# A 512-column clear on GpSimd behind each of the 3616 indirect transfers of a graph network kernel

## The chip, the cores and the metric

One Trainium2 chip, one core of it. The metric is the device time of one execution in microseconds. The engines are TensorE (PE; its weight loads are PEld in the profile), VectorE (DVE), ScalarE (ACT), GpSimd (POOL) and SyncE (SP). Two kernels are compared, before and after one change.

## The reference

A graph of 12500 nodes with 32 features and 200000 edges, sorted by destination. Layer 0 is an equivariant message layer: for each edge a small network of its weight gives 384 numbers R, which are multiplied with the features of the edge's source node and with directions, and summed at the edge's destination. Three graph convolutions follow. Cut to the core:

```python
h = jnp.maximum(_layernorm(x, axis=-1), 0.0)
# layer 0
R = jax.nn.relu(abs_distances[:, None] @ w1 + b1) @ w2 + b2
Fj = features[src]
acc = acc + _NORM[i] * jnp.einsum('euv,ef,evi,ofi->euo', Rb[..., k], Yf, Fb, C)
out = out.at[dst].add(msg)
x = x + out
# layers 1 to 3, on maximum(layernorm(x), 0)
h = x @ W
msg = h[src] * norm[:, None]
out = jax.ops.segment_sum(msg, dst, num_segments=n_nodes)
x = x + relu(conv3(relu(conv2(relu(conv1(h))))))
```

## The kernel before, in words

Each layer n keeps the node rows that its edges read in a table in DRAM, `tables[n]`, of 32, 96, 128 and 96 columns (float32 in layers 0 and 2, bfloat16 in 1 and 3). The edges are cut into groups of 1024. GpSimd fetches the source rows of a group with eight indirect transfers of 128 rows each (L768), one for each column of the index tile `idx`, into one of four slots of the buffer `rows`. These eight are called a block here. Layer 0 fetches all 196 groups so (`GATHERED[0]`); layers 1, 2 and 3 fetch 92, 100 and 64 groups, 452 in all, 3616 transfers. The other edges of layers 1 to 3 are taken as "buckets" by matmuls with one-hot matrices out of tables in SBUF (PE L2051, L2066, L2069; DVE L1597, L1626; ACT L987, L991), which run between the groups.

What a group is used for: in layer 0, ACT copies the fetched rows out of the slot (L864 to L871, the last one counts the semaphore `rows_copied`), PE makes R (L1908, L1911), DVE multiplies (L1336, L1344, L1354) and PE sums the messages with a one-hot matrix of destinations (L1926). DVE then adds the result into `accT` (L1382). In layers 1 to 3 PE sums the rows of a group directly (L2137, semaphore `group_summed`) and DVE adds them into `accT` (L1750).

The order of the work is written out by hand for each engine. `sweep` makes a first pass, a `Fori` loop over the passes between, and a last pass, peeled off on both sides; a pass holds 4 groups in layer 0, and 12, 12 and 8 in layers 1 to 3. GpSimd runs `gathers(n)`: for each group u it waits for the indices of its slot (`idx_in`, loaded by SP), then for the group four before, which used the same slot, to be read (`rows_copied` in layer 0, `group_summed` in the others), and issues the eight transfers, each counting `gathered`. So it may be up to four groups ahead. Each layer's transfers start when its table is written. SP reloads a slot's indices when `gathered` says that the transfers of that slot have landed. In the first pass of layer 0, GpSimd also clears `accT` behind its 32 transfers (L775, 12672 columns), and DVE's first addition into `accT` needs that.

The semaphore `made` counts GpSimd's constants; all who wait for it wait for at most 9.

```python
pool.wait_ge(rows_copied[r], pool.snap(turn[r]) + 1)
pool.reg_add(turn[r], turn[r], 1)
for j in range(TPG):
    col = j % 2 * KS + j // 2
    (pool.indirect_dma_start(..., tables[n], bass.IndirectOffsetOnAxis(ap=idx[:, r, col:col + 1], axis=0))
         .then_inc(gathered[r], 16))
```

Of the kernel before, what the change touches and what calls it, by code (L numbers as in the profile page):

```python
# [27 lines left out]
P = 128  # L28
# [8 lines left out]
TPG = 8  # L37
# [21 lines left out]
MSGW = TAIL0 + OUTS  # L59
SUMW = 8 * OUTS  # L60
PAD_REL = -1000.0
assert NG % UNROLL == 0 and PTAIL * KS == ETAIL and PTAIL <= P and NG == 2 * NB


# [2 lines left out]
GATHERED = [NG, 92, 100, 64]  # L67
LOOP = [(UNROLL, 0), (12, 10), (12, 8), (8, 12)]
# [64 lines left out]
def gnn_kernel(nc, x, src, dst, edge_attr, edge_weight, w1, b1, w2, b2,  # L133
               W1, B1, W2, B2, W3, B3, out):
    ctx = ExitStack()
    with ctx:
        def sb(name, shape, dt=fp32):
            return ctx.enter_context(nc.sbuf_tensor(name, shape, dt))
# [4 lines left out]
        def sem(name):  # L143
            return ctx.enter_context(nc.semaphore(name))
# [147 lines left out]
        far_shift = sb("far_shift", [P, NB + 1])  # L292
        ident = sb("ident", [P, P])
        one = sb("one", [P, 1])
        flag = sb("flag", [P, 1])
        w1c = sb("w1c", [P, 1])
        b1c = sb("b1c", [P, 1])
# [34 lines left out]
        made = sem("made")  # L332
# [118 lines left out]
        def rounds_before(n):  # L451

            return sum(GATHERED[:n]) // UNROLL
# [87 lines left out]
        def sweep(eng, body, n=0):  # L541

            body(Step(eng, 0, n), True, False)
            with eng.Fori(1, ITS[n] - 1) as it:
                body(Step(eng, it, n), False, False)
            body(Step(eng, ITS[n] - 1, n), False, True)
# [181 lines left out]
        @block.gpsimd  # L728
        def _(pool):
            nc.gpsimd.memset(xn[:, NB - 1, :], 0.0).then_inc(pads, 1)  # L730
            pool.wait_ge(pads, 1)
            nc.gpsimd.memset(attr_rows[96:NB, 1, :], 1.0).then_inc(pads, 1)
            pool.wait_ge(pads, 2)
            nc.gpsimd.iota(iota_i[:, :], pattern=[[1, WIN]], base=0, channel_multiplier=0).then_inc(made, 1)
            nc.gpsimd.iota(line_i[:, :], pattern=[[0, 1]], base=0, channel_multiplier=1).then_inc(made, 1)
            nc.gpsimd.iota(far_shift_i[:, :], pattern=[[WIN, NB + 1]], base=0, channel_multiplier=0).then_inc(made, 1)
            nc.gpsimd.memset(ident[:, :], 0.0).then_inc(made, 1)
            nc.gpsimd.memset(one[:, :], 1.0).then_inc(made, 1)
            nc.gpsimd.memset(ew_row[:, :, :], 0.0).then_inc(made, 1)
            nc.gpsimd.memset(idx[:, :, :], 0).then_inc(made, 1)  # L740
            nc.gpsimd.memset(ones_h[:, :], 1.0).then_inc(made, 1)
            pool.wait_ge(made, 8)
            nc.gpsimd.affine_select(out=ident[:, :], in_=ident[:, :], compare_op=ALU.not_equal, fill=1.0,
                                    base=0, pattern=[[-1, P]], channel_multiplier=1).then_inc(made, 1)

            turn = [pool.alloc_register(f"turn_pool{u}") for u in range(UNROLL)]

            def gathers(n):  # L750
                def body(step, first, last):
                    for u in range(shape(n, last)[0]):
                        r, use = u % UNROLL, u // UNROLL
                        pool.wait_ge(idx_in[r], step.times(step.groups // UNROLL * 16, 16 * (rounds_before(n) + use + 1)))
                        if n > 0:
                            if step.peeled and (not first or use):
                                pool.wait_ge(*when(group_summed, step, u - UNROLL, before=convs_before(n)))
                            elif not step.peeled:
                                pool.wait_ge(group_summed[r % 2], pool.snap(turn[r]) + (2 * convs_before(n) + r // 2 + 1))
                                pool.reg_add(turn[r], turn[r], 2)  # L760
                        elif last:
                            pool.wait_ge(rows_copied[r], step.it * (step.groups // UNROLL) + use)
                        elif not first:
# [4 lines that stand above are left out]
                            (pool.indirect_dma_start(rows_3[:, r, j, :] if n in (1, 3) else rows[:, r, j, 0:WIDTH[n]], None, tables[n],  # L768
                                                     bass.IndirectOffsetOnAxis(ap=idx[:, r, col:col + 1], axis=0))
                                 .then_inc(gathered[r], 16))  # L770
                    if n == 0 and first:
                        pool.wait_ge(centred, 2)
                        nc.gpsimd.memset(xn[:, NB - 1, :], 0.0).then_inc(pads, 1)
                        pool.wait_ge(prepared, 1)
                        nc.gpsimd.memset(accT[:, :], 0.0).then_inc(acc_cleared, 1)  # L775
                        pool.wait_ge(directed, 1)
                        nc.gpsimd.memset(src_b[:, (NBG - 1) * BJ:NBG * BJ], NO_SOURCE).then_inc(pads, 1)
                        nc.gpsimd.memset(dst_b[:, (NBG - 1) * BJ:NBG * BJ], -1).then_inc(pads, 1)
                if n < 2:
                    pool.wait_ge(table_out[n], 48 if n == 0 else 32)  # L780
                else:
                    if n == 3:
                        for c in range(NCH):
                            bs = blocks_of(c)
                            pool.wait_ge(middle_made, thirds_before(3) + c + 1)
                            nc.gpsimd.tensor_tensor(thirds3[:, bs, 2 * F:F3], lnA[:, bs, :], thirds3[:, bs, F:2 * F],
                                                    ALU.subtract).then_inc(thirds_made, 1)
                    for c in range(NCH - 4, NCH):
                        pool.wait_ge(chunk_out[c % 4], chunks_stored(n, c))
                for u in range(UNROLL):  # L790
                    pool.reg_mov(turn[u], 2 * (LOOP[n][0] // UNROLL - 1) if n else 0)
                sweep(pool, body, n)

            for n in range(NLAYER):
                gathers(n)
# [304 lines left out]
        def _(dve):  # L1100
# [104 lines left out]
            for n in range(4):  # L1205
# [4 lines left out]
                                     mins_by[:, h, w, :].unsqueeze(1).to_broadcast([P, KS, NB]), ALU.subtract))  # L1210
            link(v.tensor_scalar(pad_line, line[:, :], float(PTAIL), PAD_REL, ALU.is_ge, ALU.mult))
            link(v.tensor_scalar(rel_of[:, 1, 0, :, NB - 1], rel_of[:, 1, 0, :, NB - 1], pad_line, None, ALU.add))
            link(v.memset(rel_of[:, 1, 1, :, NB - 1], PAD_REL))

# [1052 lines left out]
```

## Time and profile before

| | us |
|---|---|
| median of 3 runs | 8061.44 |
| lowest and highest run | 8028.29, 8071.3 |
| the profiled execution, first to last instruction (span) | 8083.0 |
| TensorE busy | 5256.2 (65%) |
| VectorE busy | 3618.0 (45%) |
| ScalarE busy | 2730.5 (34%) |
| GpSimd busy | 3513.2 (43%) |
| mean granted TensorE clock | 0.721 |

The profiled execution's own time is known as its span alone, 8083.0 us; it lies 0.3% above the median of the three runs. "Busy" is the time in which an engine executes; in "idle before" stands what released it. "issue" means that the engine waited for nothing that the profile shows; "remote" and "another core or an unknown queue", that the releaser's record is missing. The granted clock is the share of full speed that TensorE was given. A row for GpSimd's transfer covers the making of its descriptors, not the moving of the data.

### The profile page before, as it was taken

To read this page: it belongs to the slowest core of one execution; us is meant where nothing else is said; L and a number is where in the kernel's file an instruction comes from. 1 tells how busy PE (TensorE), PEld (TensorE's weight loads), DVE (VectorE), ACT (ScalarE), POOL (GpSimd) and SP (SyncE) were. 2 spreads that over 40 slices of the span, in tenths; PEclk is the share of its full clock that TensorE was granted. 3 is DMA by queue.
4 is the path that set the end of the run, shared out by engine and by line. 5 is a ranking of instruction groups with operands and counts; after the bars stand their busy time and mean duration, and the time that the engine had idled before them with its cause. 6 is when DMAs were issued, how large, how long until landed. Compare 5 with 4: busy or idle time off the path is not lost.

```text
span 8083.0 us, 169450 instructions
## 1 busy us (share of the span) xinstructions
PE 5256.2 (65%) x62463; PEld 3511.6 (43%) x62464; DVE 3618.0 (45%) x8469; ACT 2730.5 (34%) x6550; POOL 3513.2 (43%) x3660
## 2 busy tenths in 40 slices
PE   4777677776767775554544557777777778455555
PEld 2444344443434443333333345555555556333333
DVE  6666566665656656444444442222222223333334
ACT  3333333333333333444444432222222223222222
POOL 5545445444444542444444434333333332444442
PEclk8877788787877776555555567887777788565566
DMA  2111111111111113222222221111111112222223
GB/s 66 26 26 27 24 26 27 26 26 24 27 24 26 26 25 37 59 55 55 55 55 55 55 80 55 57 56 53 56 55 53 55 55 83 68 79 81 78 82 87
DMA packets 494908, 400.37 MB, mean 50 GB/s; under 512 B 269575, under 2 KB 454828, under 8 KB 493537
## 3 DMA queue, kind: packets, MB, share of 16 engines
q10 hardware_dynamic: 146996, 207.67, 7.6%
q0 software_dynamic: 115712, 109.02, 7.1%
q1 hardware_dynamic: 231536, 74.48, 4.2%
q8 instruction: 459, 7.52, 0.4%
q14 instruction: 205, 1.68, 0.1%
HBM read 375.52 MB, written 15.29 MB: 48 GB/s over the span
## 4 chain that ended last, share of the span: by engine, by line
PE 38%; another core or an unknown queue 22%; DVE 18%; issue 17%; ACT 2%; DVEq 1%; DMA 1%; ACTq 0%; SPq 0%
PE radial L2051 14%; PE sums L1926 5%; DVE scratch L1344 4%; DVE scratch L1336 4%; PE sums L2137 4%; PE psX L2066 3%; PE psT L2066 3%; PE radial L1911 2%; PE psX L2069 2%; DVE scratch L1354 2%; PE psT L2069 1%; DVE shared L1310 1%; PE radial L2033 1%; PE radial L1908 1%
## 5 line engine op out<-in xcount | busy, mean ns | idle before, releaser
L768 POOL DMA_INDIRECT rows<-table,idx x3616 | 3486.8, 964 | 4415.6 <-PE sums L2137 2099.7
L2051 PE MATMUL radial<-arena,shared 128*32 128x96 bf16 (+1 forms) x31200 | 1469.7, 283 | 1072.6 <-issue 907.8
L2051 PEld LDWEIGHTS radial<-arena,shared 128*32 128x32 bf16 (+1 forms) x31200 | 848.1, 120 | 1551.6 <-issue 1311.4
L1926 PE MATMUL sums<-scratch,onehot 128*64 128x264 f32 (+1 forms) x9408 | 1134.5, 393 | 378.2 <-DVE scratch L1361 207.2
L1926 PEld LDWEIGHTS sums<-scratch,onehot 128*64 128x64 f32 x9408 | 818.2, 161 | 924.6 <-issue 480.7
L834 ACT ACTIVATE dist<-iota,rel 128x64 f32<-128x64 f32 (+1 forms) x2368 | 619.5, 342 | 1190.4 <-PE sums L1926 790.0
L1597 DVE TENSOR_SCALAR shared<-scratch,line 128x640 bf16<-128x640 bf16 (+1 forms) x906 | 408.3, 451 | 1367.9 <-remote 1102.7
L991 ACT CAST scratch<-radial 128x480 bf16<-128x480 f32 x860 | 470.8, 556 | 1593.4 <-remote 985.1
L1911 PE MATMUL radial<-shared 64*128 64x384 f32 x3136 | 880.9, 583 | 81.4 <-issue 77.8
L1336 DVE TENSOR_TENSOR scratch<-radial,shared 128x512 f32<-128x512 f32 x784 | 536.4, 684 | 740.4 <-remote 704.1
L1344 DVE TENSOR_TENSOR scratch<-radial,shared 128x768 f32<-128x768 f32 x784 | 741.6, 946 | 0.0
L987 ACT COPY scratch<-radial 128x384 f32<-128x384 f32 x350 | 167.3, 478 | 1275.4 <-remote 824.9
L1908 PE MATMUL radial<-shared 64*128 64x384 bf16 x1568 | 304.2, 370 | 403.2 <-DVE scratch L1344 239.6
L1626 DVE TENSOR_TENSOR shared<-radial,shared 128x480 bf16<-128x480 bf16 x860 | 345.0, 402 | 354.3 <-remote 231.3
L857 ACT ACTIVATE shared<-shared,b1c,w1c 128x512 f32<-128x512 f32 x196 | 256.9, 1311 | 657.1 <-remote 642.3
L1911 PEld LDWEIGHTS radial<-shared 64*128 64x128 f32 x3136 | 371.7, 222 | 206.1 <-issue 203.5
L1623 DVE TENSOR_TENSOR shared<-iota,shared 128x480 f32<-128x480 f32 x350 | 230.1, 657 | 394.9 <-remote 182.3
L2069 PE MATMUL psT<-shared,scratch 128*96 128x96 bf16 x2150 | 252.7, 271 | 203.0 <-issue 107.9
L2069 PE MATMUL psX<-shared,scratch 128*96 128x96 bf16 x2150 | 242.8, 264 | 187.3 <-issue 107.7
L1908 PEld LDWEIGHTS radial<-shared 64*128 64x128 bf16 x1568 | 81.9, 96 | 648.3 <-issue 321.1
L2137 PE MATMUL sums<-onehot,rows 128*128 128x80 f32 (+1 forms) x2844 | 346.5, 286 | 25.9 <-issue 24.9
L2137 PEld LDWEIGHTS sums<-onehot,rows 128*128 128x128 f32 (+1 forms) x2844 | 310.3, 196 | 77.3 <-issue 65.6
(236 smaller groups left out, 5445.4 us busy)
## 6 DMA issues: line engine op xcount, KB each, us to landing
scratch<-places_d ACTq DMA_DIRECT2D x242, 800.0 KB
rows<-table,idx POOLq DMA_INDIRECT x3616
shared<-in_edge_weight SPq DMA_DIRECT2D x390, 128.0 KB
idx<-in_src SPq DMA_DIRECT2D x451, 4.0 KB
table<-arena SPq DMA_DIRECT2D x24, 256.0 KB, 2.7
table<-arena SPq DMA_DIRECT2D x2, 1176.0 KB, 10.6
accT<-in_edge_attr SPq DMA_DIRECT2D x2, 1152.0 KB
table<-arena SPq DMA_DIRECT2D x24, 96.0 KB, 2.0
```

What stands on the lines that cost most here:

```text
L768: (pool.indirect_dma_start(rows_3[:, r, j, :] if n in (1, 3) else rows[:, r, j, 0:WIDTH[n]], None, tables[n], bass.IndirectOffsetOnAxis(ap ...
L834: ins = nc.scalar.activation(dist[:, j, 0:span], iota[:, 0:span], ACT.Abs, scale=-1.0, bias=rel[:, bass.ds(step.tile(u) + j, 1)])
L991: nc.scalar.copy(taken[n][:, h, :, :], radial[0][:, h, 0:KC * F3].rearrange("p (t f) -> p t f", f=F3)).then_inc(bucket_copied, 1)
L1336: prod = v.tensor_tensor(msg[:, h, t:t + 2, 0:2 * SEG0].rearrange("p t (m s) -> p t m s", s=16), R[:, :, 0:256].rearrange("p t (m s) -> p ...
L1344: last = v.tensor_tensor(msg[:, h, t:t + 2, SEG0 + 16 * (MUL + 1):TAIL0].rearrange("p t (n s) -> p t n s", s=16), R[:, :, 256:384].unsquee ...
L1908: nc.tensor.matmul(radial[q % 2][:, k, 0:RDIM], ones_h[half, :], bias_rows[half, :], start=True, stop=False, tile_position=(k * HID0, 0))
L1911: last = nc.tensor.matmul(radial[q % 2][:, k, 0:RDIM], hid[half, u % 2, q, :], w2n[half, 0, :], start=False, stop=True, tile_position=(k * ...
L1926: last = nc.tensor.matmul(there, onehot[:, u % 2, 4 * h + t, 0:SW], taken_from, start=(h + q + part == 0), stop=(h == 1 and q == 1 and par ...
L2051: last = nc.tensor.matmul(d, from_src[n][:, h, i, t, :], table_of(n, s), start=True, stop=True, tile_position=(0, 32 * i))
L2066: last = nc.tensor.matmul((psX if v % 2 else psT)[0:BWIN, 0:HID], to_dst[n][:, h, t, :], taken[n][:, h, t, :], start=(c + t == 0), stop=(c ...
L2069: last = nc.tensor.matmul((psX if v % 2 else psT)[0:w, 0:BWIN], taken[n][:, h, t, :], to_dst[n][:, h, t, :], start=(c + t == 0), stop=(c * ...
L2137: mm = nc.tensor.matmul(sums[0:w, u % 2, 0:CWIN], far_rows[j], (onehot if n == 2 else onehot_3)[0:counts[j], u % 2, j, 0:CWIN], start=(j = ...
```

## The change

Behind each indirect transfer GpSimd now clears a buffer of its own, `pause`, of 512 float32 columns. Every clear counts `made`, and waits for the clear before it: in the peeled passes for a constant, in the loops for a register that is counted up. Nobody reads `pause`.

```diff
+PAUSE = 512
...
+        pause = sb("pause", [P, PAUSE])
...
+            pauses = pool.alloc_register("pauses")
+
+            def pause_between(step, n, u, j):
+
+                if step.peeled:
+                    before = TPG * (sum(GATHERED[:n]) + step.it * step.groups + u) + j
+                    if before:
+                        pool.wait_ge(made, 9 + before)
+                else:
+                    pool.wait_ge(made, pool.snap(pauses))
+                    pool.reg_add(pauses, pauses, 1)
+                nc.gpsimd.memset(pause[:, :], 0.0).then_inc(made, 1)
...
                                  .then_inc(gathered[r], 16))
+                            pause_between(step, n, u, j)
...
+                pool.reg_mov(pauses, 9 + TPG * (sum(GATHERED[:n]) + LOOP[n][0]))
                 sweep(pool, body, n)
```

The instructions of PE, DVE, ACT and SP stand in the same order as before. Those of GpSimd change in all passes alike: a clear follows each transfer. In GpSimd's loop of layer 0 they stood so before, a row for each kind of instruction, with the semaphores waited for in brackets:

```order
L764 ISA [waits idx_in0]
L765 REGISTER_ALU [waits rows_copied0]
L768 DMA rows<-table,idx 128x32 x8
L764 ISA [waits idx_in1]
L765 REGISTER_ALU [waits rows_copied1]
L768 DMA rows<-table,idx 128x32 x8
```

and now, for the first half of one block (L764 to L768 of before are L778 to L782 here):

```order
L778 ISA [waits idx_in0]
L779 REGISTER_ALU [waits rows_copied0]
L782 DMA rows<-table,idx 128x32
L761 REGISTER_ALU [waits made]
L762 MEMSET pause 128x512
L782 DMA rows<-table,idx 128x32
L761 REGISTER_ALU [waits made]
L762 MEMSET pause 128x512
L782 DMA rows<-table,idx 128x32
L761 REGISTER_ALU [waits made]
L762 MEMSET pause 128x512
```

Between two transfers of a block stand now one register addition, one wait and one clear. At the end of the first pass of layer 0, ahead of the long clear of `accT`, it is:

```order
L782 DMA rows<-table,idx 128x32
L762 MEMSET pause 128x512 [waits made]
L782 DMA rows<-table,idx 128x32
L762 MEMSET pause 128x512 [waits made]
L788 MEMSET xn 128x32 [waits centred]
L790 MEMSET accT 128x12672 [waits prepared]
```

All 32 clears of the first four blocks stand ahead of the clear of `accT`.

## Rows read from the trace of the kernel before

**Rows 1.** The page: busy time by engine, and the chain's shares by engine
```profile
PE 5256.2 (65%) x62463; PEld 3511.6 (43%) x62464; DVE 3618.0 (45%) x8469; ACT 2730.5 (34%) x6550; POOL 3513.2 (43%) x3660
...
PE 38%; another core or an unknown queue 22%; DVE 18%; issue 17%; ACT 2%; DVEq 1%; DMA 1%; ACTq 0%; SPq 0%
```

**Rows 2.** GpSimd's transfers at 130:3050, 3168:4690, 4778:6770, 6888:8015; busy us, mean ns | idle
```profile
L768 POOL DMA_INDIRECT rows<-table,idx x1498 | 1439.3, 961 | 1482.0 <-ACT shared L871 1040.6 <-issue 441.4
...
L768 POOL DMA_INDIRECT rows<-table,idx x732 | 710.9, 971 | 920.4 <-PE sums L2137 604.2 <-issue 206.9 <-DMA table<-arena 109.4
...
L768 POOL DMA_INDIRECT rows<-table,idx x793 | 771.1, 972 | 1303.3 <-PE sums L2137 995.9 <-issue 307.4
...
L768 POOL DMA_INDIRECT rows<-table,idx x505 | 476.9, 944 | 654.7 <-PE sums L2137 499.6 <-issue 148.7 <-remote 6.4
```

**Rows 3.** Stretches: PE, PEld, DVE, ACT, POOL busy us (instructions), clock, DMA share, GB/s
```profile
79.70:90.30 10.60, 8.52 (x74) 5.55 (x76) 10.36 (x19) 8.91 (x24) 10.60 (x2) 1.00 0.21 54
90.60:96.60 6.00, 5.78 (x49) 3.26 (x45) 5.82 (x10) 4.43 (x13) 4.72 (x5) 1.00 0.16 35
96.60:130.50 33.90, 7.40 (x31) 3.74 (x30) 2.62 (x7) 0.95 (x4) 25.64 (x27) 0.60 0.11 18
130.50:160.00 29.50, 21.52 (x153) 12.51 (x152) 20.81 (x39) 10.99 (x33) 7.07 (x8) 0.82 0.34 78
```

**Rows 4.** The same view inside one block each of layers 0, 1, 2 and 3
```profile
1044.00:1049.00 5.00, 4.82 (x44) 3.29 (x42) 5.00 (x9) 2.74 (x9) 3.77 (x4) 1.00 0.12 18
1049.00:1055.20 6.20, 3.13 (x18) 1.55 (x14) 2.42 (x4) 2.93 (x7) 3.77 (x4) 1.00 0.19 48
...
3914.80:3922.40 7.60, 1.72 (x14) 0.91 (x14) 0.86 (x3) 0.56 (x1) 4.79 (x5) 0.59 0.16 28
...
5568.20:5571.90 3.70, 3.23 (x61) 2.58 (x60) 0.82 (x2) 0.00 (x0) 2.86 (x3) 1.00 0.47 152
5571.90:5579.50 7.60, 3.57 (x22) 0.90 (x21) 0.55 (x1) 0.75 (x2) 4.85 (x5) 0.71 0.19 52
5579.50:5588.20 8.70, 8.47 (x87) 7.38 (x88) 2.11 (x4) 4.51 (x14) 0.00 (x0) 0.67 0.02 1
...
7317.00:7325.70 8.70, 2.45 (x21) 1.23 (x21) 1.05 (x3) 0.56 (x1) 5.66 (x6) 0.63 0.28 78
```

**Rows 5.** Two blocks of layer 2 in order of time: start, us, what [idle before]
```profile
5510.19 0.97 POOL L768 DMA_INDIRECT rows<-table,idx  x1 [11.73 <-PE sums L2137]
5512.98 0.94 POOL L768 DMA_INDIRECT rows<-table,idx  x1 [1.82 <-issue]
...
5568.20 0.97 POOL L768 DMA_INDIRECT rows<-table,idx  x1 [11.78 <-PE sums L2137]
5569.48 0.94 POOL L768 DMA_INDIRECT rows<-table,idx  x1 [0.31 <-issue]
...
5516.55 0.27 PE L2051 MATMUL radial<-arena,shared 128*32 128x128 f32 x1 [0.33 <-issue]
...
5572.46 0.45 PE L2051 MATMUL radial<-arena,shared 128*32 128x128 f32 x5 [1.02 <-issue]
```

**Rows 6.** ACT in order of time, start of layer 2
```profile
4799.11 0.58 ACT L912 COPY accT<-radial 128x512 f32<-128x512 f32 x1 [4.34 <-remote]
...
4818.07 0.58 ACT L912 COPY accT<-radial 128x512 f32<-128x512 f32 x1 [10.61 <-remote]
```

**Rows 7.** GpSimd's memsets, by form; busy us, mean ns | idle
```profile
L775 POOL MEMSET accT<- 128x12672 f32 x1 | 10.7, 10681 | 0.0
...
L739 POOL MEMSET shared<- 128x1024 f32 x1 | 1.0, 952 | 0.0
...
L737 POOL MEMSET ident<- 128x128 f32 x1 | 0.2, 205 | 0.0
```

**Rows 8.** DVE: its first addition into accT, and the operation L1597 (min/median/max ns)
```profile
106.52 0.21 DVE L1382 TENSOR_TENSOR accT<-accT,psT 33x64 f32 x1 [10.10 <-remote]
...
L1597 DVE TENSOR_SCALAR shared<-scratch,line x906: 369/386/670, 3238.2 to 8055.5; 128x640 bf16<-128x640 bf16 x112, 128x640 f32<-128x640 bf16 x70
```

## The prediction, on record before the run

> **What bounds the kernel now.** I read the page first. No engine is full: TensorE is busy 65% of the span, GpSimd 43%, and 17% of the chain of waits is "issue", time in which an engine waited for nothing that the profile shows [rows 1]. The largest group of the page is not a matmul but GpSimd's indirect transfer at L768, 3616 of them, about 0.96 us each. They come in blocks of eight, one block for each group of 1024 edges.
>
> The second view is GpSimd's groups in four stretches, one per layer [rows 2]. A stretch divided by its number of blocks gives the time per group: layer 0 2920 us for 1498/8 = 187 groups, 15.6 us; layer 1 1522 for 91.5, 16.6; layer 2 1992 for 99.1, 20.1; layer 3 1127 for 63.1, 17.9. GpSimd is ahead: a block takes 8 x 1.25 = 10 us (0.94 to 0.97 busy plus 0.30 idle), and the rest of the period it waits for the group whose rows it will overwrite, four groups back: 1040.6 us for ACT L871 in layer 0, that is 5.6 us per group, and 6.6, 10.0 and 7.9 us for PE L2137 in the others. So at first sight the transfers are hidden and nothing that is done to them matters.
>
> The third view says otherwise: busy time of the engines in stretches chosen by where GpSimd's blocks lie. Near the start there is a run of 32 transfers without a wait, 90.6 to 130.5 us [rows 3]. For its first 6.0 us PE is busy 5.78 and DVE 5.82; in the next 33.9 us PE is busy 7.40, DVE 2.62 and ACT 0.95; once the run has ended all three work again (21.52, 20.81 and 10.99 of 29.5 us). What stopped them is not load on the DMA engines: their share is 0.11 in the dead stretch and 0.34 in the living one behind it. Nor is it GpSimd computing: in the 10.60 us ahead, which one long memset fills on GpSimd (L775, 10681 ns), PE is busy 8.52, DVE 10.36, ACT 8.91 [rows 3, 7]. Single blocks of eight show the same in small [rows 4]. In layer 0 the first 5 us of a block are full (PE 4.82 of 5.00) and the next 6.2 us are half empty (3.13); in layer 1 the 7.6 us from the fourth transfer until about 1.5 us after the last hold 1.72 us of PE; in layer 2 3.57, with 8.47 of 8.70 in the stretch behind; in layer 3 2.45 of 8.7. PE is idle in these stretches for 3.1, 5.9, 4.0 and 6.2 us per group, and the other engines with it. That is where the "issue" time is, and it is the true bound: **something fills up while transfers are issued back to back, and empties when they stop.**
>
> Two details show a store that fills. PE's gaps "issue" begin at 5571.4, 3.2 us behind the block's start at 5568.20; in the block whose first transfer (5510.19) is followed by 1.82 us of idleness, they begin at 5516.2, 3.2 us behind the second transfer (5512.98) and 6.0 behind the first [rows 5]. A pause of 1.8 us had wiped out what the first transfer had filled. And at the start of layer 2, in a run of 32, ACT's waits at L912, for PE's next piece, grow from 4.34 to 10.61 us within 20 us [rows 6]: a backlog that grows with the run.
>
> **The change, part by part.** (1) 3616 clears of 512 columns on GpSimd, one behind each transfer. The trace has clears of 128 and 1024 columns, 205 and 952 ns [rows 7]; between them 747/896 = 0.83 ns per column, so 205 + 384 x 0.83 = 0.53 us each. The bounds are these two rows, 0.2 and 0.95. I take 0.53, since both rows are the same operation and type. (2) In the loops, one register addition and one wait on the semaphore of the clear before. The addition and wait that precede each block today leave the gap to the second transfer at 0.31 [rows 5] instead of 0.30, so I cost them at nothing, at most 0.1 us. What is queued behind that wait is the next transfer, but the awaited clear lies a transfer back and is over. (3) The transfers themselves, SP's index loads and all other engines' instructions keep their order.
>
> So the spacing goes from 1.25 to about 1.79 us (0.94 to 0.97, plus 0.30, plus 0.53), a block from 10.0 to 14.3 us, and GpSimd's busy time from 3513 to about 5430 us. GpSimd's own cover: its waits per group (5.6, 6.6, 10.0, 7.9 us) exceed the 4.2 us added, so it can keep today's pace, and a block is asked for four groups ahead. But 14.3 us is the new floor of a group. If a transfer with its clear cost 1.95 us or more, layer 0 would be bound by it (15.6 us). At the start, the 32 clears of the first four blocks add 17 us ahead of the long clear at L775; it then ends near 107 instead of 90.3, and the first addition into accT, which stands at 106.52 [rows 8], waits a microsecond or so more. Layers 1 to 3 start with four blocks but sum after one, so each start is later by 4.2 us at most, 13 us together; I count nothing, since the same starts also hold runs of 32 transfers whose dead time should shrink.
>
> (4) What the pause gives back. Take the store's content as 1 when PE stops. In layers 1 to 3 it is full after about 3 transfers, so a transfer of 0.95 us with its 0.3 us gap fills about 0.33; the stretches of [rows 4] are alive again about 1.5 us after the last transfer (in layer 2 PE is busy 8.47 of 8.70 us), so a free microsecond empties at least 0.67. Then a transfer alone fills 0.33 + 0.3 x 0.67 = 0.53, and the new gap of 0.83 us empties 0.56. The balance is just about even: the store should no longer fill, or fill slowly. This rests on a clear leaving the store alone, as L775 does. So much of the dead time should return. I take half of it, since the balance is so close and PE's granted clock falls with the stall (in layer 2 from 1.00 ahead of it to 0.71 in it and 0.67 behind it) and need not come back at once. Half of 3.1, 5.9, 4.0, 6.2 is 1.6, 3.0, 2.0, 3.1 us per group, capped by the floor of 14.3 at 1.3, 2.3, 5.8, 3.6. **Sum:** layer 0 196 x 1.3 = 255; layer 1 92 x 2.3 = 212; layer 2 100 x 2.0 = 200; layer 3 64 x 3.1 = 198; together 865 us. All of it returned would be 255 + 212 + 400 + 230 = 1097; a fifth (0.6, 1.2, 0.8, 1.2) 118 + 110 + 80 + 77 = 385. The profiled execution has a span of 8083, 22 us above the median of 8061; 8083 - 865 - 22 = 7196, said as **7200 us**; all returned 6960, a fifth returned 7680.
>
> **Rivals.** *The stall lasts as long as the block (slower).* If what matters is that GpSimd is inside a run of transfers and a gap of 0.83 us is as useless as one of 0.30, the dead stretch grows by 4.2 us at the same low activity. Idle share there by [rows 4]: 0.50, 0.77, 0.53, 0.72. Loss 2.1, 3.3, 2.2, 3.0 us per group: 412 + 304 + 220 + 192 = 1128 us, about 9190. It decides if the gap needed to empty the store lies above 0.83 us; the trace shows only that 0.30 is too short and 1.82 enough. Against it: [rows 5] and the balance above. For it: the wait in [rows 6] reaches 10.61 us, and its growth may not be turned by half a microsecond. 0.19.
> *A fixed price per transfer.* If each transfer takes its 0.9 us from the others whenever it comes, eight take as much as before; or the clear does not push the transfers apart, being done inside their idle gaps. Then nothing changes but the start: 8050 to 8080. Against: PE is busy through the first 3 to 5 us of each block. 0.08.
> *The clears stand in DVE's way.* The only large DVE operation beside them that the transfers themselves lengthen is L1597, median 386 and maximum 670 ns over 906 [rows 8]. If each met a clear and waited for all of it, 906 x 0.53 = 480 us; clears fill 4.2 of some 17 us, so a quarter of them wait for half a clear, 60 us, on an engine that is busy 45%. It would show only where nothing else is won: 8120 to 8150. 0.03. The Trainium skill (SBUF — State Buffer, "The single rule") has this rule: DVE's two-port forms, `tensor_scalar` among them, and GpSimd hold one port pair exclusively, and the later of the two blocks fully. By that rule these waits come to pass; in layer 0, whose loop is tensor_tensor and reduce, nothing would wait. The rows of the memset L775 agree for layer 0's operations; for L1597 no row shows a clear.
>
> **How the numbers follow.** Half or more of the dead time returned (6850 to 7400): 0.45. A smaller part (7400 to 8020): 0.25. Fixed price 0.08, DVE 0.03, the longer stall 0.19. Within 0.5% of 8061 (8021 to 8102, about what a measurement of this kernel can tell from no change): 0.08. Faster 0.70, slower 0.22. The range reaches from 6850, a little under the floor of all returned because a steadier PE also keeps its clock, to 8150; only the longer stall, 0.19, and a sliver below lie outside. The forecast's own range is 6850 to 7680.
>
> **What would show it.** Right: the transfers 1.7 to 1.9 us apart; clears of 0.5 us; in a block of layer 2 PE busy over 70% behind the fourth transfer; granted clock above 0.72 in the mean; GpSimd's waits for ACT L871 and PE L2137 near nothing in layers 0 and 1, because it is now what sets the pace; "issue" below 17% of the chain. Wrong: dead stretches of 11 us behind the first 3 to 5 us of each block (the longer stall); the old 5 to 6 us spread over a longer block with the same period (fixed price); transfers with clears at 1.95 us or more.

## The result, and the profile after

The changed kernel takes 6420.66 us (median of 4 runs, 6418.82 to 6429.66), the kernel before in the same job 8066.37; the ratio is 0.7976, 95% interval 0.7956 to 0.7997. The profiled execution has a span of 6417.5 us against 8083.0, 1665.5 us less. The direction and the mechanism were forecast, the size was not: 7200 was the forecast, 6850 the lower end of the range.

The page of the changed kernel (its lines are 14 to 16 further down, so L768 is L782, L871 is L887, L2137 is L2153): busy time, the granted clock in 40 slices, the chain's shares, and four groups of instructions.

```profile
PE 4556.8 (71%) x62463; PEld 3336.9 (52%) x62464; DVE 3632.7 (57%) x8469; ACT 2714.1 (42%) x6550; POOL 5536.7 (86%) x7276
...
PEclk9888888888888888755555555888888899655555
...
POOL 59%; issue 35%; POOLq 2%; PE 2%; DVE 1%; DMA 1%; ACT 0%; DVEq 0%; SPq 0%; ACTq 0%
...
L782 POOL DMA_INDIRECT rows<-table,idx x3616 | 3535.1, 978 | 794.6 <-POOL pause L762 484.5
L762 POOL MEMSET pause<- 128x512 f32 x3616 | 1983.8, 549 | 2.5
...
L2153 PE MATMUL sums<-onehot,rows 128*128 128x80 f32 (+1 forms) x2844 | 402.3, 314 | 515.8 <-DMA rows<-table,idx 489.2
...
L880 ACT COPY shared<-rows 128x192 f32<-128x192 f32 x196 | 89.3, 456 | 1494.4 <-DMA rows<-table,idx 1493.1
```

Against [rows 1], GpSimd is busy 5536.7 us instead of 3513.2, and it is the chain: 59% of it is transfers and clears. TensorE is busy 4556.8 instead of 5256.2 us for the same 62463 matmuls, VectorE's busy time is unchanged. The transfers cost what they did (978 ns; 961 to 972 in the first three stretches of [rows 2]); a clear costs 549 ns. Now the others wait for the transfers' data: ACT L880 1493.1 us, PE L2153 489.2 us, both for `rows<-table,idx`. Before, GpSimd waited for them.

GpSimd's transfers by layer, in the stretches 110 to 2650, 2736 to 3980, 4037 to 5440 and 5513 to 6380 us, as in [rows 2] (busy, mean ns, idle before):

```profile
L782 POOL DMA_INDIRECT rows<-table,idx x1522 | 1453.2, 955 | 265.8 <-POOL pause L762 239.9 <-issue 25.9
...
L782 POOL DMA_INDIRECT rows<-table,idx x731 | 711.2, 973 | 204.4 <-issue 113.1 <-POOL pause L762 91.3
...
L782 POOL DMA_INDIRECT rows<-table,idx x797 | 815.0, 1023 | 194.2 <-issue 102.9 <-POOL pause L762 91.3
...
L782 POOL DMA_INDIRECT rows<-table,idx x510 | 496.3, 973 | 93.3 <-POOL pause L762 61.5 <-issue 31.8
```

The time per group is again the stretch over its blocks: 2540 us for 1522/8 = 190 groups is 13.35; then 1244 for 91.4, 13.61; 1403 for 99.6, 14.08; 867 for 63.8, 13.60. Before it was 15.59, 16.63, 20.10 and 17.86. No wait for PE L2153 or ACT L887 is left in these rows: GpSimd never waits for a slot to be read.

Next the stretches: PE, PEld, DVE, ACT, POOL busy us with instructions, granted clock, DMA share, GB/s. First the start of layer 0, whose long clear of `accT` now runs from 91.40 to 102.08 us; then one whole block in each of layers 0 to 3; last the stretch of that block of layer 2 behind its fourth transfer.

```profile
79.70:91.30 11.60, 10.53 (x76) 6.13 (x72) 11.39 (x21) 9.75 (x28) 10.46 (x15) 1.00 0.24 60
...
108.30:140.00 31.70, 26.30 (x215) 17.35 (x213) 25.53 (x50) 13.40 (x37) 28.62 (x39) 0.89 0.38 78
...
1010.80:1024.10 13.30, 9.91 (x75) 5.71 (x73) 9.37 (x18) 5.49 (x16) 11.96 (x17) 0.87 0.17 30
3306.30:3319.70 13.40, 6.66 (x163) 5.27 (x163) 8.03 (x28) 7.18 (x12) 12.10 (x17) 0.63 0.34 80
4811.90:4825.70 13.80, 11.89 (x167) 10.93 (x167) 4.26 (x8) 3.52 (x10) 12.54 (x16) 0.75 0.18 42
5907.80:5921.40 13.60, 9.31 (x195) 6.96 (x187) 6.34 (x20) 4.12 (x8) 12.28 (x17) 0.50 0.34 90
4816.80:4825.70 8.90, 8.90 (x155) 7.94 (x154) 4.26 (x8) 3.52 (x10) 8.11 (x10) 0.84 0.16 39
```

The run of transfers behind 108.30 us is the one in which before everything stood still for 33.9 us ([rows 3], PE busy 7.40, DVE 2.62). Here in 31.7 us, with GpSimd inside transfers and clears for 28.62 of them, PE is busy 26.30 and DVE 25.53. In layer 2 PE is busy for all of the 8.90 us behind the fourth transfer; before it was 3.57 of 7.6 [rows 4]. Over a whole group it is busy 11.89 of 13.80 us, before 15.27 of 20.00 (5568.20 to 5588.20, the sum of the three stretches in [rows 4]). The DMA engines' share behind 108.30 us is higher (0.38), not lower.

### The profile page after: what moved, and what is told of

Read it like the earlier page. It is cut to its first block, busy times and chain, and to the rows that moved or that the text cites. A ratio compares the mean times of both kernels' runs of the same rounds, so it can differ in the third digit from the quotient of the medians.

```text
span 6417.5 us, 179150 instructions
## 1 busy us (share of the span) xinstructions
PE 4556.8 (71%) x62463; PEld 3336.9 (52%) x62464; DVE 3632.7 (57%) x8469; ACT 2714.1 (42%) x6550; POOL 5536.7 (86%) x7276
## 3 DMA queue, kind: packets, MB, share of 16 engines
q0 software_dynamic: 115712, 109.02, 9.7%
## 4 chain that ended last, share of the span: by engine, by line
POOL 59%; issue 35%; POOLq 2%; PE 2%; DVE 1%; DMA 1%; ACT 0%; DVEq 0%; SPq 0%; ACTq 0%
POOL pause L762 31%; POOL rows L782 28%; POOLq L761 2%; PE radial L2209 0%; DMA table<-arena 0%; PE radial L2067 0%; PE radial L2222 0%; PE psX L2082 0%; POOLq L760 0%; PE sums L2153 0%; DMA rows<-table,idx 0%; DMA xn<-in_x 0%; DVE rows L1827 0%; PE radial L2008 0%; ACT rows L1103 0%
## 5 line engine op out<-in xcount | busy, mean ns | idle before, releaser
L782 POOL DMA_INDIRECT rows<-table,idx x3616 | 3535.1, 978 | 794.6 <-POOL pause L762 484.5
L762 POOL MEMSET pause<- 128x512 f32 x3616 | 1983.8, 549 | 2.5
L2067 PE MATMUL radial<-arena,shared 128*32 128x96 bf16 (+1 forms) x31200 | 1021.7, 277 | 198.9 <-issue 95.2
L1942 PE MATMUL sums<-scratch,onehot 128*64 128x264 f32 (+1 forms) x9408 | 1009.1, 362 | 25.2 <-DVE scratch L1377 14.1
L2067 PEld LDWEIGHTS radial<-arena,shared 128*32 128x32 bf16 (+1 forms) x31200 | 719.2, 119 | 378.5 <-issue 169.5
L1927 PE MATMUL radial<-shared 64*128 64x384 f32 x3136 | 785.6, 582 | 0.0
L2153 PE MATMUL sums<-onehot,rows 128*128 128x80 f32 (+1 forms) x2844 | 402.3, 314 | 515.8 <-DMA rows<-table,idx 489.2
L880 ACT COPY shared<-rows 128x192 f32<-128x192 f32 x196 | 89.3, 456 | 1494.4 <-DMA rows<-table,idx 1493.1
L2153 PEld LDWEIGHTS sums<-onehot,rows 128*128 128x128 f32 (+1 forms) x2844 | 365.5, 223 | 569.0 <-issue 566.2
L1326 DVE TENSOR_TENSOR shared<-arena,rows 128x576 f32<-128x576 f32 x196 | 148.7, 759 | 755.6 <-ACT shared L887 446.7
L1766 DVE TENSOR_TENSOR accT<-accT,sums 96x80 f32 (+1 forms) x256 | 60.3, 236 | 897.1 <-PE sums L2153 723.9
L1352 DVE TENSOR_TENSOR scratch<-radial,shared 128x512 f32<-128x512 f32 x784 | 535.3, 683 | 13.4 <-issue 13.4
L1642 DVE TENSOR_TENSOR shared<-radial,shared 128x480 bf16<-128x480 bf16 x860 | 344.0, 401 | 50.1 <-PE psT L2085 17.6
```

What stands on the lines that cost most here:

```text
L762: nc.gpsimd.memset(pause[:, :], 0.0).then_inc(made, 1)
L1352: prod = v.tensor_tensor(msg[:, h, t:t + 2, 0:2 * SEG0].rearrange("p t (m s) -> p t m s", s=16), R[:, :, 0:256].rearrange("p t (m s) -> p ...
L1927: last = nc.tensor.matmul(radial[q % 2][:, k, 0:RDIM], hid[half, u % 2, q, :], w2n[half, 0, :], start=False, stop=True, tile_position=(k * ...
L1942: last = nc.tensor.matmul(there, onehot[:, u % 2, 4 * h + t, 0:SW], taken_from, start=(h + q + part == 0), stop=(h == 1 and q == 1 and par ...
L2067: last = nc.tensor.matmul(d, from_src[n][:, h, i, t, :], table_of(n, s), start=True, stop=True, tile_position=(0, 32 * i))
L2153: mm = nc.tensor.matmul(sums[0:w, u % 2, 0:CWIN], far_rows[j], (onehot if n == 2 else onehot_3)[0:counts[j], u % 2, j, 0:CWIN], start=(j = ...
```

## Experiments

The theory, **S**: something fills while GpSimd is inside a transfer and empties in the time between two transfers; when it is full, the other engines stand still. Rivals: **W**, any other instruction or wait between two transfers breaks the stall; **M**, only the mean rate of transfers over a group counts; **D**, what fills it are the descriptors. All of the following runs are variants of the changed kernel unless said otherwise. One execution each, except where an interval is given, so differences of 1 or 2% between them are not read; the kernel before, beside them on the same chip, took 7997 to 8083 us.

| run | free time behind a transfer, us | time, us |
|---|---|---|
| before | 0.30 | 8066 |
| clear_1 | 0.30 | 8172 |
| clear_256 | 0.49 | 7163 |
| clear_384 | 0.60 | 6438 |
| clear_448_timed | 0.65 | 6326 |
| the change, 512 columns | 0.70 | 6421 |

"Free time" is what lies between the end of a transfer and the start of the next within a block (the clear included): the median spacing of the transfers within a block, taken over the whole trace, less the 0.95 us of a transfer.

**One column.**

```diff
-PAUSE = 512
+PAUSE = 1
```

> One column instead of 512: the same instructions, waits and order, but a clear of about 0.1 us. Theory S (a store fills while GpSimd makes descriptors and empties in the time between transfers): the free time between two transfers is 0.1 + 0.16 = 0.26 us, less than the 0.30 of before, so the stalls are back and the time is 7900 to 8300. Rival W (any other instruction, or the wait, between two transfers breaks what stalls the others): transfers 1.2 us apart without stalls, GpSimd's pace is 10 us per group and the engines' own work decides: 5700 to 6300.

Measured: 8172 us. GpSimd in layer 0 in order of time, and whom it waited for:

```profile
1000.13 0.94 POOL L782 DMA_INDIRECT rows<-table,idx  x1 [0.19 <-issue]
1001.06 0.12 POOL L762 MEMSET pause<- 128x1 f32 x1
1001.37 0.94 POOL L782 DMA_INDIRECT rows<-table,idx  x1 [0.19 <-issue]
```

```profile
POOL rows L782 <- PE sums L2153: 2057.1, 237, 21.0
POOL rows L782 <- ACT shared L887: 1089.9, 171, 16.5
```

All the instructions, waits and register additions of the change are there, and nothing is gained. A clear of one column takes 0.12 us and leaves 0.19 us of idleness, so the free time is 0.30 (1001.07 to 1001.37), not the 0.26 that I had expected: exactly that of before. GpSimd again waits 2057 and 1090 us for its slots, as it did before (in [rows 2] 1040.6 for ACT, and 604.2 + 995.9 + 499.6 = 2099.7 for PE). W falls.

**256 columns.**

```diff
-PAUSE = 512
+PAUSE = 256
```

> 256 columns: a clear of 0.31 us, transfers about 1.42 us apart, 0.47 us free between them against 0.70 with 512 columns and 0.30 without a clear. Theory S: somewhere between, depending on where filling and emptying balance; if the balance lies below 0.47, no stalls, and GpSimd's pace of 11.5 us per group gives 5700 to 6000; if above, 6500 to 7500. Rival W: as with one column, 5700 to 6000.

Measured: 7163 us, in between. GpSimd's waits:

```profile
POOL rows L782 <- PE sums L2153: 983.1, 209, 10.5
...
POOL rows L782 <- ACT shared L887: 401.5, 71, 9.3
```

They are down to less than half of clear_1's. A pace of 11.5 us per group was open to it and is not reached.

**The clears behind the block.**

```diff
-                            pause_between(step, n, u, j)
+                            if j == TPG - 1:
+                                for k in range(TPG):
+                                    pause_between(step, n, u, k)
```

> The same eight clears of 512 columns per group, all behind the eighth transfer: the same work for GpSimd, transfers again 1.25 us apart within a block. Theory S: the stalls of before return; GpSimd's pace of 14.5 us per group is below the period of before, so 7900 to 8200. Rival M (what counts is the mean rate of transfers over a group, the clears only slow GpSimd down): 6400 to 6800.

Measured: 7986 us beside 7997 of the kernel before. GpSimd in layer 0 and its waits:

```profile
1014.49 0.94 POOL L782 DMA_INDIRECT rows<-table,idx  x1 [0.30 <-issue]
1015.42 5.17 POOL L762 MEMSET pause<- 128x512 f32 x8
1020.89 0.95 POOL L782 DMA_INDIRECT rows<-table,idx  x1 [0.30 <-issue]
```

```profile
POOL rows L782 <- PE sums L2155: 704.6, 203, 10.5
```

DVE's longest wait in layer 0, from 500 to 3000 us:

```profile
DVE nodes L1388 <- remote: 499.9, 148, 5.4
```

GpSimd has the same 3616 clears to do as in the change, 1937 us, and issues as many transfers per group, but the time is that of before. Two things make it so. In layers 1 to 3 the stalls are back: GpSimd waits 704.6 us for PE, which it never does in the change, and the groups take 16.5, 19.8 and 17.6 us, where GpSimd's own pace would allow 15.2. There M falls, and it isn't the load of the clears that helps. In layer 0 the time can't tell: eight clears in a chain take 5.17 us, so GpSimd's own pace is 15.2 us per group, not the 14.5 that I had expected, nearly the 15.6 of before, and GpSimd waits for nobody. That the stall is there too is seen only in the others: DVE waits 499.9 us on "remote", which are late signals of PE (see the bound, below).

**The clears in twos.**

```diff
-                            pause_between(step, n, u, j)
+                            if j % 2:
+                                for k in (j - 1, j):
+                                    pause_between(step, n, u, k)
```

> Two clears of 512 columns behind every second transfer: runs of two transfers 1.25 us apart, then 1.25 us free. Theory S: two transfers don't fill the store (it took three to four), and the pause empties what they filled: 6350 to 6600, as with a clear behind each. If the store empties only at the end of a run and by more than the free time says, slower than that. Rival W: every second gap is as before; 7000 or more.

Measured: 6937 us, above what I gave it. GpSimd in layer 0 and its waits:

```profile
1001.67 0.95 POOL L782 DMA_INDIRECT rows<-table,idx  x1 [0.29 <-issue]
1002.92 0.95 POOL L782 DMA_INDIRECT rows<-table,idx  x1 [0.30 <-issue]
1003.88 1.20 POOL L762 MEMSET pause<- 128x512 f32 x2
1005.23 0.95 POOL L782 DMA_INDIRECT rows<-table,idx  x1 [0.15 <-issue]
```

```profile
POOL rows L782 <- issue: 1117.3, 3602, 67.8
...
POOL rows L782 <- DMA idx<-in_src: 28.9, 1, 28.9
```

There is no wait for PE or ACT among them, so GpSimd alone sets the pace: whatever two transfers close together do to the others is over before it costs time. It agrees with S, but does not show that pairs are harmless, since a slower GpSimd would hide a small stall. What I had left out is GpSimd's own pace. The second clear waits for the first, and the two take 1.20 us instead of twice 0.54; a pair takes 3.56 us (1001.67 to 1005.23), four of them 14.2, and 452 groups of that 6440. Over whole layers the groups took 14.5 to 15.1 us, a little more still. The miss was in the price of GpSimd's block.

**384 and 448 columns.**

```diff
-PAUSE = 512
+PAUSE = 384
```

> 384 columns: a clear of about 0.44 us, transfers 1.55 us apart, 0.60 us free; GpSimd's pace 12.4 us per group against 13.3 with 512. Theory S: with 256 columns (0.47 free) groups of layers 1 and 3 still took 15.8 and 17.0 us, with 512 (0.70) none stalled. If the balance lies below 0.60, the pace decides: about 6000 to 6150. If it lies between 0.60 and 0.70, stalls are left in layers 1 and 3: 6300 to 6800. Rival: the gain with 512 columns comes from something else than free time, then no smooth passage from 7163 to 6420 would be seen.

> 448 columns: a clear of about 0.49 us, transfers 1.60 us apart, 0.65 us free, pace 12.9 us per group. Theory S: 6200 to 6250 if no stalls are left, up to 6500 if some are in layers 1 and 3.

Measured: 6438 and 6320 us. GpSimd's waits with 384 columns:

```profile
POOL rows L782 <- PE sums L2153: 290.6, 137, 6.3
```

With 0.60 us free 137 waits for PE are left, with 0.49 there were 209, so the passage is smooth. 448 columns beat 512: the stalls are nearly gone at 0.65 us already, and what lies above is only GpSimd's pace. It was then run four times:

> The kernel with 448 columns again, now timed: 6320 as in its one look, within 20 us; 1.5% below the 6420 of 512 columns, since it differs by GpSimd's pace alone (8 x 0.057 = 0.46 us per group, 452 groups, 206 us at most).

Measured: 6326.06 us (4 runs), ratio to before 0.7852, interval 0.7824 to 0.7881, against 0.7976 of the change. GpSimd's waits for PE:

```profile
POOL rows L782 <- PE sums L2153: 19.6, 17, 2.3
```

**Descriptors or transfers.** This one is made from the kernel before, without clears. The kernel leaves out the second half of the indices: both halves of a transfer's rows are fetched by the first 64.

```diff
-            return step.times(step.groups // UNROLL * 16 * TPG, 16 * TPG * (rounds_before(n) + u // UNROLL + plus))
+            return step.times(step.groups // UNROLL * 32 * TPG, 32 * TPG * (rounds_before(n) + u // UNROLL + plus))
...
-                            (pool.indirect_dma_start(rows_3[:, r, j, :] if n in (1, 3) else rows[:, r, j, 0:WIDTH[n]], None, tables[n],
-                                                     bass.IndirectOffsetOnAxis(ap=idx[:, r, col:col + 1], axis=0))
-                                 .then_inc(gathered[r], 16))
+                            for half in (slice(0, 64), slice(64, P)):
+                                (pool.indirect_dma_start(rows_3[half, r, j, :] if n in (1, 3) else rows[half, r, j, 0:WIDTH[n]], None, tables[n],
+                                                         bass.IndirectOffsetOnAxis(ap=idx[0:64, r, col:col + 1], axis=0))
+                                     .then_inc(gathered[r], 16))
```

> The kernel before, no clears, each transfer of 128 rows split in two of 64 (the second half fetches by the first half's indices, so other rows are read, as many as before). Theory D (what fills the store are the descriptors, and GpSimd writes them faster than they are taken): if a transfer of 64 rows takes GpSimd nearly as long as one of 128, the descriptors come at half the rate and the stalls vanish; PE stays busy inside the runs, and GpSimd's pace of 16 transfers, 16 to 20 us per group, sets the time: 7600 to 9500. Theory T (each transfer of whatever size takes the others' time, since GpSimd is inside transfers three quarters of the time): stalls go on through the whole run, PE's share in it as low as 0.3 to 0.5, and the time is above 9500.

Measured: 13402 us. The transfers, and two stretches of layer 0 (columns as above); the first of them holds the last 17 transfers of two blocks of 16 that follow each other without a wait, the second is the 20 us behind them:

```profile
L769 POOL DMA_INDIRECT rows<-table,idx x7232 | 6602.4, 913 | 6612.4 <-issue 3314.1 <-PE sums L2138 1974.9 <-ACT shared L872 1165.5
```

```profile
2996.50:3016.70 20.20, 0.00 (x0) 0.00 (x0) 0.00 (x0) 0.00 (x0) 15.32 (x17) 0.50 0.05 7
3016.70:3036.80 20.10, 12.63 (x102) 8.41 (x103) 13.20 (x28) 5.82 (x17) 0.00 (x0) 0.72 0.05 14
```

For 20.2 us no engine but GpSimd executes a single instruction, while the DMA engines' share is 0.05. A transfer of 64 rows takes GpSimd 0.91 us, hardly less than one of 128, so the rows come at half the rate; the stall is worse than ever. D falls as far as it is about rows. But the page counts 115712 packets for the 3616 transfers of before and 231424 for the 7232 here, 32 for each transfer in both. So what counts is GpSimd's time inside transfers, or something that each transfer brings whatever its size, and these packets may be it.

What the others wait for is seen in two rows of the same trace, in order of time:

```profile
2985.12 0.27 PE L1941 MATMUL psT<-ident,nodes 128*33 128x128 f32 x1 [0.31 <-issue]
...
3023.45 0.21 DVE L1383 TENSOR_TENSOR accT<-accT,psT 33x64 f32 x1 [33.29 <-remote]
```

DVE's addition waits for the semaphore `nodes_turned`, which PE L1941 alone counts. By the trace the matmul ended at 2985.39, and the count came at 3023.32, 38 us later and 6.6 us behind the end of GpSimd's last transfer; three other counts of PE, for work that ended between 2984.8 and 2996.0, came within 0.2 us of it.

The same with the clear of 512 columns behind each of the 7232 transfers, made from the changed kernel (what `pause_between` counts is adapted too):

```diff
+                            for h, half in enumerate((slice(0, 64), slice(64, P))):
...
+                                     .then_inc(gathered[r], 16))
+                                pause_between(step, n, u, 2 * j + h)
```

> The 7232 transfers of 64 rows, with a clear of 512 columns behind each (rows fetched as in the run halves: others than the indices say). Theory S with a price per transfer: free time 0.70 us per transfer of 0.90, so no stalls, and GpSimd's pace of 16 x 1.60 = 25.6 us per group is the time: 452 x 25.6 plus some 400 us outside, 11900 to 12300, less than the 13402 without clears though GpSimd has 3900 us more to do. Rival (in halves the engines are slow for another reason, the number of landings or semaphore counts): the clears add to 13402, 14000 or more.

Measured: 12196 us, inside the expectation. The chain's shares:

```profile
POOL 63%; issue 33%; POOLq 2%; DVE 1%; PE 1%; DMA 0%; ACT 0%; DVEq 0%; SPq 0%
```

GpSimd has 3947 us of clears to do that the run before has not, and still the kernel is 1206 us faster, with GpSimd as its chain. Free time behind each transfer cures this one too.

**A width for each layer.**

```diff
-PAUSE = 512
+PAUSE = [384, 448, 384, 448]
...
-                nc.gpsimd.memset(pause[:, :], 0.0).then_inc(made, 1)
+                nc.gpsimd.memset(pause[:, 0:PAUSE[n]], 0.0).then_inc(made, 1)
```

> Clears of 384, 448, 384 and 448 columns in layers 0 to 3. In the uniform runs the groups took 12.68 us in layer 0 and 13.53 in layer 2 with 384 columns, 13.59 and 13.40 in layers 1 and 3 with 448. If each layer keeps its own balance, the sum against 448 everywhere (6320) is 196 x 0.31 + 100 x 0.20 = 81 us less: 6240. Rival: the layers' times differ between runs by more than that, then 6300 or more.

> Clears of 320, 448, 416 and 448 columns. In layer 0 320 columns give 0.53 us free and a pace of 1.49 x 8 = 11.9 us per group. Theory S with a balance for layer 0 below 0.53: 0.6 us less per group than with 384, 6150 to 6200. If layer 0's balance lies between 0.53 and 0.60, stalls are back in it: 6250 to 6500 (256 columns gave 13.95 us per group).

Measured: mixed_a 6265.02 us (6243.73 to 6269.03), ratio 0.7768, interval 0.7736 to 0.7799, the fastest of all, 61 us below 448 columns everywhere where I had expected 81; mixed_b (320, 448, 416, 448) 6414.61, ratio 0.7952, 0.7918 to 0.7986. They differ above all in layer 0. GpSimd's transfers there, from 500 to 2500 us, in mixed_a:

```profile
L782 POOL DMA_INDIRECT rows<-table,idx x1270 | 1227.0, 966 | 223.6 <-POOL pause L762 156.9 <-issue 66.8
```

and in mixed_b:

```profile
L782 POOL DMA_INDIRECT rows<-table,idx x1192 | 1176.0, 987 | 372.3 <-ACT shared L887 165.1 <-POOL pause L762 123.4 <-issue 83.8
```

2000 us hold 1270/8 = 159 groups with 384 columns, 12.6 us each, and 149 with 320, 13.4 us each, though GpSimd could go faster; it waits for ACT L887 again. In layer 0 GpSimd waits for ACT 71 times with 0.49 us of free time (clear_256), 49 times with 0.54 (mixed_b) and not once with 0.60, so its balance lies between 0.54 and 0.60. In layers 1 and 3, 0.60 was a little short (126 of the 137 waits of clear_384); of mixed_a, with 0.65 there, 34 are left:

```profile
POOL rows L782 <- PE sums L2153: 42.8, 34, 3.8
```

## Why the prediction was wrong in size

**The bound.** Right, and now shown: not load, not GpSimd computing, but transfers back to back. clear_1, clear_block (in layers 1 to 3) and halves hold it against three rivals, D only as far as it is about rows. The "issue" and "remote" waits of before were symptoms, and the second of them says more than I read from it. Before, 1193 waits are "remote", 5570 us in all, and each of them is a wait of DVE, ACT or (once) GpSimd for a semaphore that PE alone counts; for DVE the count came 5.9 us behind the end of the matmul in the median, for ACT 6.1. With the change 271 such waits are left, 378 us. Over all of PE's counts before, the median lag is 3.5 us while GpSimd is in a run of transfers and 0.02 us otherwise; for the counts of DVE and of ACT it is 0.01 us in both (some counts are missing from the trace, so these are medians of what is there). TensorE also issues late: ahead of L2051 it sat idle for 907.8 us on "issue" before, and 95.2 with the change. So what stands still first is TensorE, and DVE and ACT wait for it. A matmul's end is modelled in the profile, so the runs don't tell whether the matmul or its signal is late.

**The rivals.** The longer stall (0.19) did not come; its point of decision was put at 0.83 us of free time, the measured one is near 0.6. The fixed price per transfer did not come either. DVE's waits for the clears did, at about the size given: L1597 has become

```profile
L1613 DVE TENSOR_SCALAR shared<-scratch,line x906: 371/460/1292, 2777.9 to 6391.2; 128x640 bf16<-128x640 bf16 x112, 128x640 f32<-128x640 bf16 x70
```

that is, its maximum went from 670 to 1292 ns [rows 8], and its mean from 451 to 503 (the median, 386 to 460, mixes two forms); 906 times 52 ns is 47 us, against the 60 of the text, on an engine that is busy 57% of the span; its share in the time was not measured by itself. With clears of one column the median is 387 ns and the maximum 780. In layer 0 the two large operations take what they took: L1336 and L1344 684 and 946 ns before, 683 and 949 with the change. The rule of the Trainium skill (SBUF — State Buffer, section "Who interferes with whom", "The single rule") agrees with the trace here, in the layers for which it was cited.

**The balance of filling and emptying (step 4).** It came out even (0.53 filled, 0.56 emptied at 0.83 us) and I took half of the dead time as returned. The measured free time is 0.70, less than I had, and the balance was still on the good side. The store empties faster than 0.67 per microsecond; that was a lower bound, and I took it as the value. With the balance measured near 0.6 us, the text's own terms (0.33 + 0.3 x r = 0.6 x r) give an estimate of 1.1. This is the step that failed first: half of the dead time was booked, and all of it came back. All returned, capped by my own floor, was 1097 us, 232 more than the 865 of the sum.

**The floor of 14.3 us (step 1 and the spacing).** The clear cost 0.54 as reckoned (0.53), but the idle 0.30 us ahead of a transfer did not stay:

```profile
4811.85 0.95 POOL L782 DMA_INDIRECT rows<-table,idx  x1 [0.16 <-POOL pause L762]
4812.81 0.54 POOL L762 MEMSET pause<- 128x512 f32 x1
4813.51 0.95 POOL L782 DMA_INDIRECT rows<-table,idx  x1 [0.16 <-POOL pause L762]
```

A clear starts at once when the transfer ends, and the next transfer stands 0.16 us behind it. The spacing is 1.66 us, not 1.79; a block needs 13.3 us, not 14.3. In all layers GpSimd's pace is what stopped the gain. In layers 0, 1 and 3 the floor had capped it at 255 + 212 + 230 = 697 us; 391 + 275 + 264 = 930 were gained there, 233 more.

**The dead time of layer 2.** I took 4.0 us per group, PE's idleness behind the fourth transfer of one block. Layer 2 gained 20.10 - 14.08 = 6.0, and 191 us more than even my "all returned". The whole layer before and with the change (columns as above):

```profile
4778.00:6770.00 1992.00, 1519.97 (x18194) 1128.85 (x18197) 430.16 (x824) 543.75 (x1616) 771.08 (x793) 0.79 0.19 55
...
4037.00:5440.00 1403.00, 1198.01 (x18851) 1061.11 (x18852) 457.89 (x852) 561.64 (x1672) 1256.82 (x1593) 0.88 0.28 80
```

The block was no bad sample: PE is idle 472 of 1992 us, 4.8 per group, and 4.7 in the block. What was wrong is that only idle time was taken as lost. PE's idleness fell from 4.8 to 2.1 us per group, and its busy time from 15.3 to 12.0, for about as many matmuls (184 and 189 a group). The granted clock is a part of it at most: in the two single groups given above PE executes 170 and 167 matmuls in 15.27 and 11.89 us busy, at 0.74 and 0.75. So a stall also stretches the time that counts as busy.

**What I counted at nothing.** Layers 1 and 2 begin earlier after their predecessor. GpSimd's first transfers of these layers:

```profile
2735.96 0.95 POOL L782 DMA_INDIRECT rows<-table,idx  x1 [68.24 <-issue]
...
4037.02 0.95 POOL L782 DMA_INDIRECT rows<-table,idx  x1 [48.55 <-issue]
```

They waited 68.2 and 48.6 us for the tables where before it was 109.4 [rows 2] and, of the "issue" of layer 2, 83.0 (the longest wait of that kind in the waits view). Ahead of layer 3 the time between the transfers fell too, from 110.0 to 66.9 us, and behind the last transfer of all from 59.5 to 33.3. Together with 0.8 us at the start this makes 145 us that the sum had at nothing. I take them to come from engines that no longer stall in the last groups of a layer; no run shows it by itself.

**The signs.** Of those named, four came as said: PE busy over 70% behind the fourth transfer in layer 2 (8.90 of 8.90), the mean clock above 0.72, GpSimd's waits for L887 and L2153 gone, clears of 0.5 us. The spacing, 1.66, lies just below the 1.7 to 1.9 named. "issue" rose to 35% of the chain instead of falling below 17%: the chain now runs along GpSimd, which is idle only 14% of the span, so the chain's view calls "issue" also time in which GpSimd is inside the instruction before. It is no sign of a stall here, and was badly chosen. The clear of `accT` ended at 102 instead of 107, by the shorter spacing.

**The sum, put right.** From the first transfer of a layer to the end of its last: 3024.5 - 2633.3 = 391; 1526.9 - 1252.0 = 275; 2000.2 - 1409.3 = 591; 1134.7 - 871.0 = 264. With the 145 us outside this is 1666 of 1665.5 us. Against the 865 of the forecast: 232 from the half, 233 from the floor, 191 from layer 2, 145 from between and behind the layers. No one of the four would have closed the gap; with the half alone mended the forecast would still be 6960.

**The clock.** I expected it to rise with steadier work. Its mean went from 0.72 to 0.76. By layer, in the stretches above, it rose from 0.80 to 0.88 in layer 0 and from 0.79 to 0.88 in layer 2, and fell from 0.55 to 0.52 in layer 1 and from 0.60 to 0.52 in layer 3. There the gain is large all the same: in these two layers it is returned time, not clock. What the higher clock is worth in the other two was not measured by itself.

**What stays open:** what the store is. The runs show that it is filled by GpSimd's time in indirect transfers or by something each transfer brings in equal measure at 64 and 128 rows, such as its 32 packets, that about 0.6 us of a clear with the idleness around it empties it, and that the DMA engines' load is not it. TensorE's counts come late while it is full, but what delays them, whether it is a way that they share with the transfers' own signals or with the writing of descriptors, was not tried. Nor was any other filling of the pause than a clear, or a wait alone.

## What to carry to other kernels

An engine that is never waited for can still hold up all others: compare the other engines' busy time inside and outside of its bursts before calling its work hidden. Indirect transfers issued back to back from GpSimd are such a burst; here 0.6 to 0.65 us free behind each, most of it a clear, returned 22% of the kernel, and an idle engine's spare time is the place to pay for it. Once it is paid, the spacing is the pace, so the shortest pause that still keeps the engines alive is the best one, and it differs by layer. And in a program on one core, a wait that the profile puts down to "remote" need not come from outside: see which engine counts that semaphore, and when it had done its work.

## What the runs showed of the hardware

- Runs of transfers 1.20 to 1.25 us apart slow every other engine after 3 to 5 us: PE 7.40, DVE 2.62 and ACT 0.95 us busy in 33.9 us (before), and 0 instructions in 20.2 us on PE, DVE and ACT (halves), with the DMA engines' share at 0.11 and 0.05.
- In such runs TensorE's semaphore counts come late: 3.5 us behind the end of the matmul in the median before, 38 us in the case shown from halves. Those of DVE and ACT come 0.01 us behind their instructions in the median, in runs of transfers as outside.
- A free time of 0.30 us behind a transfer is useless, whether idle or partly filled with a clear of one column (8172 us); 0.49 returns half (7163), 0.60 to 0.65 nearly all of it (6438 and 6326, with 137 and 17 waits for PE left).
- An indirect transfer costs GpSimd 0.91 us for 64 rows and 0.96 for 128, and makes 32 packets in both: its price is one of the instruction, hardly of the rows.
- A clear follows a transfer without idleness, and shortens the idleness ahead of the next transfer from 0.30 to 0.16 us. Two clears that wait for each other take 1.20 us, not 1.09.
